# Building the token lists of a mixture of experts: one-hot rows for three tiles at a time, or one by one with a scalar per partition

## The reference, cut to what matters

```python
def _L0_ffn_ref(x, gate_w, gate_b, w1, b1, w2, b2, gamma, beta):
    gate_logits = x @ gate_w + gate_b
    topk_vals, topk_idx = jax.lax.top_k(gate_logits, K)          # K = 2 of E = 16
    topk_w = jax.nn.softmax(topk_vals, axis=-1)
    h = jax.nn.relu(jnp.einsum('bsh,ehf->bsef', x, w1) + b1)
    expert_out = jnp.einsum('bsef,efh->bseh', h, w2) + b2
    sel = jnp.take_along_axis(expert_out, topk_idx[:, :, :, None], axis=2)
    moe = jnp.sum(topk_w[..., None] * sel, axis=2)
    y = x + moe
    # layer norm of y, times gamma, plus beta
```

## Time and profile before

| what | us |
|---|---|
| median of 3 runs | 2831.32 |
| lowest, highest | 2830.65, 2836.65 |
| the profiled execution | 2835.38 |
| its span, first to last instruction | 2833.8 |
| VectorE busy in the span | 1833.3 (65%) |
| TensorE matmuls busy | 2213.0 (78%) |
| first comparison of the loop starts | 2272.77 |
| first operation behind the loop starts on VectorE | 2303.87 |

### The profile page before, as it was taken

How to read it: one execution, slowest core, us unless ns; L and a number is a source line. 1 busy time by engine, 2 the same in 40 slices (tenths; PEclk the granted TensorE clock), 3 DMA queues, 4 the chain that set the end, 5 groups by cost and what they waited for, 6 DMA issues and landing times. The chain is left out here.

```text
span 2833.8 us, 54434 instructions
## 1 busy us (share of the span) xinstructions
PE 2213.0 (78%) x11635; PEld 1734.9 (61%) x11636; DVE 1833.3 (65%) x4388; ACT 926.9 (33%) x2258; POOL 1854.4 (65%) x1934
## 2 busy tenths in 40 slices
PE   1738777777777777758888888888888479999986
PEld 0526555555555555446666666666666269999975
DVE  5658677777777776566666666666666565555546
ACT  0512333333333333302222222222222144444436
POOL 0257777777777777467777777777777126666644
PEclk9969999999999999879999999999999689999998
DMA  3745555555555555265565655565665345555545
GB/s 66 221 134 144 145 147 147 146 148 145 146 145 146 145 146 146 72 214 161 158 159 159 162 155 162 155 162 155 163 159 159 90 129 101 103 101 105 103 79 187
DMA packets 275132, 401.58 MB, mean 142 GB/s; under 512 B 91280, under 2 KB 187943, under 8 KB 275049
## 3 DMA queue, kind: packets, MB, share of 16 engines
q0 software_dynamic: 102496, 253.89, 36.5%
q1 hardware_dynamic: 128037, 100.76, 13.4%
q10 hardware_dynamic: 44532, 46.18, 5.0%
HBM read 346.42 MB, written 54.62 MB: 142 GB/s over the span
## 5 line engine op out<-in xcount | busy, mean ns | idle before, releaser
L983 POOL DMA_INDIRECT gathered<-table,idx x1568 | 1488.3, 949 | 488.4 <-issue 447.6
L1312 PE MATMUL psA_e<-scaled,hotf 128*128 128x260 f32 x3136 | 749.0, 393 | 42.0 <-issue 36.9
L1312 PEld LDWEIGHTS psA_e<-scaled,hotf 128*128 128x128 f32 x3136 | 589.7, 193 | 132.1 <-issue 46.0
L1183 ACT ACTIVATE scaled<-t_e 128x32 f32<-128x32 f32 x196 | 45.0, 230 | 741.1 <-DVE t_e L1045 735.2
L1715 POOL DMA_INDIRECT moe_d<-xscaled,xtarget x113 | 179.3, 1586 | 129.1 <-DVE xtarget L1659 52.3
L1056 DVE TENSOR_TENSOR scaled<-gathered,psDW_e 128x2048 f32<-128x2048 f32 x98 | 223.6, 2282 | 25.6 <-ACT psDW_e L1184 25.6
L1049 DVE TENSOR_TENSOR hotf<-psA_e,code_r 128x1024 f32<-128x1024 f32 x196 | 239.7, 1223 | 0.0
L1056 DVE TENSOR_TENSOR scaled<-gathered,psW_e 128x2048 f32<-128x2048 f32 x98 | 223.6, 2281 | 22.1 <-ACT psW_e L1184 22.1
L1696 PE MATMUL xpsO<-w,hidT 128*128 x904 | 218.4, 385 | 10.5 <-DVE hidT L1648 9.8
L1687 PEld LDWEIGHTS xpsH<-xxT,w1e 128*128 128x128 f32 x1808 | 220.5, 193 | 6.2 <-ACT xxT L1616 0.4
L1687 PE MATMUL xpsH<-xxT,w1e 128*128 128x128 f32 x1808 | 221.2, 276 | 0.0
(11 more groups left out here) (327 smaller groups left out, 3372.5 us busy)
## 6 DMA issues: line engine op xcount, KB each, us to landing
w<-codes_d SPq DMA_DIRECT2D x196, 256.0 KB
gathered<-table,idx POOLq DMA_INDIRECT x1584
w<-in_L_ffn_w ACTq DMA_DIRECT2D x8, 2048.0 KB, 19.0
xb<-in_L_ffn_b SPq DMA_DIRECT2D x113, 128.0 KB, 3.3
table<-acc POOLq DMA_DIRECT2D x49, 130.0 KB, 2.7
table<-acc ACTq DMA_DIRECT2D x49, 130.0 KB, 2.8
xnT_d<-xnT ACTq DMA_DIRECT2D x49, 128.0 KB, 1.9
w<-xnT_d SPq DMA_DIRECT2D x49, 128.0 KB, 3.7
```

Source lines behind the costliest of these rows:

```text
L983: pool.indirect_dma_start(out=G[:, q, k, :], out_offset=None, in_=table, in_offset=bass.IndirectOffsetOnAxis(ap=idx[:, q, k:k + 1], axis=0 ...
L1183: act.activation(scaled[:, par, :, C:GW], t[:], ACT.Exp).then_inc(s["weights"], 1)
L1312: ins = pe.matmul(psA[:, q, 0:GW], hotf[:, q, k, :], scaled[:, par, k, :], start=(k == 0), stop=(k == KT - 1))
```

## The change

Each one-hot row is made by a `tensor_scalar` operation of its own. For `places` it compares `across` with the tile number, an operand from memory, and multiplies by the token's number, a second one, in the same operation. For `slots` it compares with the slot number. ScalarE's part in the loop is gone, as is its semaphore, and TensorE waits for each pair's two rows instead of for each group's `slots` and each tile's `tokens`.

```diff
@@ -1449,11 +1449,6 @@
             act.wait_ge(s["b1T"], 1)
             act.activation(b1T[:].rearrange("p e k -> p (e k)"), psB[:, 0:NX * FF // P], ACT.Copy)
-            for g, group in enumerate(groups):
-                act.wait_ge(s["places"], g + 1)
-                for m, i in enumerate(group):
-                    pair = places[:, g % 2, 2 * m:2 * m + 2, :]
-                    act.activation(pair, pair, ACT.Copy, scale=number[:, i:i + 1]).then_inc(s["tokens"], 1)
@@ -1509,12 +1504,12 @@
             for g, group in enumerate(groups):
-                n, lo, hi = 2 * len(group), group[0], group[-1] + 1
                 if g >= 2:
                     dve.wait_ge(s["listed"], groups[g - 2][-1] + 1)
-                for into, width, at, told in ((places, XT, tile, "places"), (slots, P, slot, "slots")):
-                    dve.tensor_tensor(into[:, g % 2, 0:n, :], across[:, 0:width].rearrange("p (m f) -> p m f", m=1).to_broadcast([P, n, width]),
-                                      at[:, lo:hi, :].rearrange("p t (k f) -> p (t k) f", f=1).to_broadcast([P, n, width]), ALU.is_equal).then_inc(s[told], 1)
+                for m, i in enumerate(group):
+                    for k in range(2):
+                        dve.tensor_scalar(places[:, g % 2, 2 * m + k, :], across[:, 0:XT], tile[:, i, k:k + 1], number[:, i:i + 1], ALU.is_equal, ALU.mult).then_inc(s["places"], 1)
+                        dve.tensor_scalar(slots[:, g % 2, 2 * m + k, :], across, slot[:, i, k:k + 1], None, ALU.is_equal).then_inc(s["slots"], 1)
@@ -1551,11 +1546,11 @@
             for g, group in enumerate(groups):
-                pe.wait_ge(s["slots"], g + 1)
                 for m, i in enumerate(group):
                     r = rows_of(i)
-                    pe.wait_ge(s["tokens"], i + 1)
                     for k in range(2):
+                        pe.wait_ge(s["places"], 2 * i + k + 1)
+                        pe.wait_ge(s["slots"], 2 * i + k + 1)
                         ins = pe.matmul(psL[:, 0:XT], slots[0:r, g % 2, 2 * m + k, :], places[0:r, g % 2, 2 * m + k, :],
                                         start=(i == 0 and k == 0), stop=(i == NT - 1 and k == 1), skip_group_check=True)
                     ins.then_inc(s["listed"], 1)
```

More of the change, by code:

```diff
@@ L1431, in order @@
         psE = ctx.enter_context(nc.psum_tensor("opsE", [P, 512], F32))
-        s = {n: sem("o_" + n) for n in ("consts", "steps", "both", "ranked", "pads", "slots", "places", "tokens", "listed", "b1", "b1T", "extra",
+        s = {n: sem("o_" + n) for n in ("consts", "steps", "both", "ranked", "pads", "slots", "places", "listed", "b1", "b1T", "extra",
                                         "upto", "column", "past", "owner")}
```

## The result

The changed kernel is slower. Its median is 2843.37 us (2841.23 to 2847.02, 6 runs) against 2832.70 us for the kernel before (2829.21 to 2836.65, 6 runs), 10.7 us more; the ratio is 1.0039 with a 95% interval from 1.0028 to 1.0049, which is 7.9 to 13.9 us. 2845.8 us was forecast, 14.5 us more than a kernel before at 2831.3. The profiled execution took 2841.23 us, with a span of 2839.6 us, 5.8 us above the one of the earlier trace rows.

A forecast was written before the change was run, and what follows sets the result against it. VectorE was taken to bound stage `order`: 98 pairs at 456 ns plus 0.87 us make a 45.6 us loop against 31.10, +14.5 us. On a median of 2831.3 that gives 2845.8 us, range 2839.5 to 2851.0.

The forecast's parts named there:

- What bounds the stage: Stage `order`: VectorE sets its end, with TensorE having 0.77 us to spare; loop time goes through to the end.
- The kernel before at 276 ns a pair: `order` loop before the change: a pair costs 251 ns of columns and 25 ns of shared fixed parts, 276 ns.
- The price of a one-hot: VectorE in the changed loop: a `slots` row costs 202 ns, a `places` row 254 ns, 456 ns a pair.
- The second operand is free: Rival for VectorE's rows: both fixed parts are 135 ns, a pair 396 ns, +8.6 us, 2839.9 us; chance 0.06.
- one column a cycle: Rival on VectorE: comparison or odd 113 columns miss the double rate, 126 ns more a pair, +26.8 us; chance 0.03.
- operands for nothing: Rival on VectorE: operand reads hide behind the operation before, 274 ns a pair, -3.4 us, 2827.9 us; chance 0.04.
- it just keeps up at 0.50: TensorE in the loop: at granted clock 0.50 it needs 440 ns a pair against VectorE's 456.
- TensorE becomes the bound: Rival in the loop: TensorE stays at 0.50, waits stretch 440 to about 500 ns a pair, +18.8 us; chance 0.05.
- The pauses: VectorE's waits in the loop before, 3.2 us in all: put to ScalarE's late start and 0.50 clock, zero after.
- The sum: Whole kernel: +14.5 us from the loop, on a median of 2831.3 us, gives 2845.8 us.
- if the stages behind it change by more than 1 us: Sign of being wrong: the stages behind the `order` loop change by more than 1 us.
- The other two signs: Signs of being wrong in the loop: `places`-to-`slots` distance under 200 ns, or VectorE pausing for TensorE.

## Why the prediction was right, point by point

- What bounds the stage, VectorE: right. The changed loop has no pause of VectorE, ScalarE and TensorE are off its path, and `experts` starts as much later, counted from the start of `order`, as the loop is longer.
- The kernel before at 276 ns a pair without its pauses: right. The trace has distances of 0.782 us behind the comparisons of 678 columns and 0.868 behind those of 768 that no wait lengthens, which is 1.650/6 = 275 ns a pair.
- The price of a one-hot: right in mechanism, a little too high in size. 202 and 254 ns were forecast, 195 and 249 measured; the fixed parts are 68, 128 to 129 and 190 ns with no, one and two operands, where 74, 135 and 195 were taken. Part of it is that distances were read from starts given to 10 ns; line 489 itself gives 195 (eight distances of 328 to 329 ns in that trace) and not 197, and why that is 5 ns more than here is open. It is the only such line with two operands that ran; with one there are more than the text ahead of the prediction lists (648, 1032, 1477 and 1533 among them). The error is 12 ns a pair, 1.2 us, and the small operations took 0.7 instead of 0.87, which has a wait of 0.15 in it: 44.2 us for 45.6 forecast.
- "The second operand is free" falls by the five distances above, "one column a cycle" by the 249 ns, "operands for nothing" by 127 against 188.
- TensorE: that it just keeps up at 0.50 was needed in earnest. The clock, at 1.00 once, fell again from 2282.6 to 2289.5, where the forecast had only its start at 0.50 in mind. It needed 426 ns a pair there (440 were taken) against VectorE's 444. The two matmuls between groups 3 and 4 had put it 1.6 us behind, and at 0.50 it won back only 18 ns a pair; at group 6 VectorE came to its wait of line 1508 just 0.35 us after group 4's last matmul had ended in the trace. No pause came, but the rival that TensorE becomes the bound was nearer than its 0.05 says.
- The pauses: their total, 3.2 us, was right, and that they vanish. Their cause was right in half. Beside the 1.85 us the prediction named the clock as well as ScalarE's late start, but then let all pauses go with the late start ("and thus the pauses"), and that step failed. With ScalarE on time 1.35 of 1.85 us stayed, only the higher clock removed them, and about 1.4 us of pauses in the later groups depend on neither. The forecast was not touched, as none of them is left in a loop slowed to 444 ns a pair.
- The sum: +14.5 us was forecast, +13.06 came in the stage and +10.7 (7.9 to 13.9) in the medians, so that the forecast lies just above the interval. The error of the step is 1.4 us; the other 2.4 us lie outside `order`, where the prediction allowed 2 for noise. That the forecast of 2845.8 us is only 2.4 above the 2843.37 measured is in part luck: the median of the kernel before came out 1.4 us above the 2831.3 that it started from.
- The signs: "if the stages behind it change by more than 1 us" was named as a sign of being wrong, and it came, with 6.4 us less in `experts`. It was badly chosen. Three profiles of the one kernel before differ by 3.4 us in that stage, so a change of 1 us in it can't tell anything. The other two signs stayed away: a `places` row is 249 ns ahead of its `slots` row, and VectorE makes no pause for TensorE.
- The rule on small operations that was cited from the Trainium skill (VectorE: DVE Perf Modes, on the TRN2 errata) pointed the right way. The Trainium skill's figure of about 75 ns for the fixed part (Vector Engine (DVE) Microarchitecture Reference, 5.2) fits operations with constants, 68 ns here; with operands from memory the runs show 128 to 129 and 190.

## What to carry to other kernels

Price a row of independent VectorE operations by the distance from start to start. Here it was 68 ns and the columns, and 61 ns more for each scalar that is read from memory, one number a partition; the second arithmetic operation was free. Splitting a comparison of six rows of 113 or 128 columns into single ones at the double rate saved 59 and 67 ns of columns a row and cost about 178 and 116 ns of fixed part each (two operands and one), so rows this short are better left together, and the operation that was fused into them belonged to an engine with time to spare. Before crediting a change with a few us of the total, compare stages in several profiles: another stage here moved by as much on its own.

## What the runs showed of the hardware that was not expected

- The durations of the same operation on VectorE grew through the changed loop, from 0.33 to 0.38 us for `places`, while the distances stayed at 249 ns. In the second profile of the same kernel they did not grow (mean 0.327 instead of 0.354 us), at the same distances. The duration in such a row says little of what an operation costs, and operations overlap by 0.105 us on average in the first profile (354 against 249 and 300 against 195 ns), more than the few tens of ns told ahead of the prediction.
- TensorE's granted clock fell to 0.50 in the middle of the changed loop, at 2282.6, after a stretch with 1.55 of 2.00 us busy, and was back at 1.00 by 2289.5, with pairs at 426 ns without a wait before that.
- 24 matmuls of 128 columns, done 33 us before the next stage begins, went with 476 and 483 us for that stage, where three profiles of the kernel before have a mean of 468.2. Those are of other runs, and beside the kernel before of the same runs only about 3 us are left in the one that ran more than once. No view of the profile explains it.
- ScalarE was held for 24.2 to 26.0 us by issuing the last four of its six loads (2 MB each, the rows of line 1449), and how long it was held differed by 1.8 us between executions.
